# Triangle layers with channels innermost, a mask shared between two engines, packed expert weights

## The reference

```
x += triangle(L0)(ln(x));  t += experts(F0)(ln(t))     16 experts, each mixes its 8 best tokens of 512
x += triangle(L1)(ln(x));  t += recurrence(R1)(ln(t))  sigmoid(Wx + V y), batch norm first
x += row scan(SC)(ln(x));  t += recurrence(R2)(ln(t))  new row = row + relu(conv(previous))
x += triangle(L3)(ln(x));  t += experts(F3)(ln(t))     best 2 of 8 experts per token
```

```
a = sigmoid(zn @ Wga + bga) * (zn @ Wla + bla)      (L1: times mask[i, j] as well)
b = sigmoid(zn @ Wgb + bgb) * (zn @ Wlb + blb)      (L1: times mask[i, j] as well)
k[i, j, c] = sum over m of a[.., m, c] * b[.., m, c]
out = sigmoid(zn @ Wgo + bgo) * (layernorm(k) @ Wlo + blo)
```

## Time and profile before

| | us |
|---|---|
| median of three runs | 572.27 |
| lowest, highest | 569.99, 575.90 |
| the profiled execution, as timed | 572.75 |
| its span, first to last instruction | 570.9 |
| PE / DVE / ACT / POOL busy | 442.5 / 364.1 / 238.3 / 244.8 |

### The profile page before, as it was taken

One profiled execution on the slowest core, in us unless ns is written; L12 is line 12 of the kernel. 1 busy time (PEld: TensorE's weight loads), 2 busy tenths in 40 slices (PEclk: granted clock), 3 DMA queues, 4 the chain that ended last, 5 costly groups with the idle time before them and its releaser, 6 DMA issues.

```text
span 570.9 us, 8797 instructions
## 1 busy us (share of the span) xinstructions
PE 442.5 (78%) x3116; PEld 340.7 (60%) x3116; DVE 364.1 (64%) x1215; ACT 238.3 (42%) x573; POOL 244.8 (43%) x309
## 2 busy tenths in 40 slices
PE   3698876985898765997489976799589857909996
PEld 2356753674447642996279974499345756806664
DVE  4888584819795576006924458500978498398885
ACT  1487555311675554573620005476379533200000
POOL 2598196002483494000420004100359297119995
PEclk9989989768798989799669997899789985558999
DMA  9300000000000000000000000000000000001223
GB/s 165 71 2 1 1 1 1 1 2 0 1 1 1 2 0 1 1 1 2 1 1 2 1 1 1 1 2 1 1 1 2 0 2 1 0 0 20 38 38 56
DMA packets 34107, 6.04 MB, mean 11 GB/s; under 512 B 33644, under 2 KB 33772, under 8 KB 34029
## 3 DMA queue, kind: packets, MB, share of 16 engines
q1 hardware_dynamic: 34062, 5.46, 5.5%
HBM read 3.36 MB, written 2.10 MB: 10 GB/s over the span
## 4 chain that ended last, share of the span: by engine, by line
PE 49%; DVE 32%; POOL 9%; ACT 5%; issue 2%; DMA 1%; SPq 1%; DVEq 0%; POOLq 0%
PE psum L1283 7%; DVE moments L293 6%; DVE ab L672 5%; PE psum L1045 5%; PE psum L1044 5%; PE psum L557 4%; DVE ab L660 4%; PE psum L401 4%; POOL z L339 3%; POOL x_cols L737 3%; PE psum L1456 3%; POOL gate L732 3%; DVE z L303 3%; PE psum L1434 2%; PE psum L568 2%
## 5 line engine op out<-in xcount | busy, mean ns | idle before, releaser
L401 PE MATMUL psum<-ident,z 128*128 128x128 f32 x256 | 55.7, 360 | 42.2 <-POOL z L339 42.2
L401 PEld LDWEIGHTS psum<-ident,z 128*128 128x128 f32 x256 | 39.0, 185 | 70.3 <-POOL z L339 57.8
L527 PE MATMUL psum<-wp_L,z_t 64*128 64x320 f32 x384 | 66.8, 483 | 3.3 <-ACT z_t L324 2.1
L339 POOL TENSOR_TENSOR z<-z,stats 128x496 f32<-128x496 f32 (+1 forms) x40 | 41.5, 1038 | 59.2 <-DVE z L303 59.2
L293 DVE BATCH_NORM_STATS2 moments<-x_cols 128x6 f32<-128x64 f32 x448 | 61.8, 211 | 4.2 <-POOL x_cols L737 3.9
L324 ACT ACTIVATE z_t<-psum 128x512 f32<-128x512 f32 x56 | 40.1, 721 | 38.2 <-PE psum L401 37.9
L336 POOL MEMSET z<- 128x16 f32 x32 | 4.0, 127 | 117.5 <-DVE z L303 117.5
L527 PEld LDWEIGHTS psum<-wp_L,z_t 64*128 64x128 f32 x384 | 35.3, 199 | 30.2 <-issue 26.0
L339 POOL TENSOR_TENSOR z<-x_cols,stats 128x512 f32<-128x512 f32 x24 | 25.1, 1050 | 61.0 <-DVE stats L299 60.8
L1136 ACT ACTIVATE ab<-psum,mv 128x128 f32<-128x128 f32 x112 | 41.2, 368 | 19.2 <-PE psum L1045 8.7
L1045 PE MATMUL psum<-ab,R_vt 128*128 128x128 f32 x224 | 48.5, 300 | 0.0
(11 more groups left out here) (250 smaller groups left out, 927.2 us busy)
## 6 DMA issues: line engine op xcount, KB each, us to landing
x_cols<-in_x_dram SPq DMA_DIRECT2D x16, 128.0 KB, 3.0
out_dram<-x_cols SPq DMA_DIRECT2D x32, 64.0 KB, 1.9
par<-in_par_dram SPq DMA_DIRECT2D x1, 644.5 KB
w<-in_w_dram SPq DMA_DIRECT2D x1, 264.0 KB
w<-in_w_dram SPq DMA_DIRECT2D x1, 256.0 KB
mask<-in_mask_dram SPq DMA_DIRECT2D x1, 64.0 KB
row<-in_row_dram SPq DMA_DIRECT2D x1, 3.3 KB
w2l<-in_w2l_dram SPq DMA_DIRECT2D x1, 2.0 KB
```

The lines of the kernel that those rows point to most:

```text
L339: pool.tensor_tensor(Z4[:, r, :, 0:c], values[:, r, :, 0:c], RSTD[:, q].unsqueeze(3).to_broadcast([N, SQ, G, c]), ALU.mult).then_inc(L.s[" ...
L401: m = pe.transpose(bank(b % 2)[:, k * N:(k + 1) * N], block_of(Z)(4 * b + k), ident[:, :])
L527: m = pe.matmul(bank(slot_bank(s) + h, 2 * 5 * C), ZT[rows, s, :], wp[l][rows, :, :], start=True, stop=True)
```

## The change

Four things, in the diff below.

The triangle factors lie in two planes, a and b, each (g, s, c) with the channel innermost: DVE writes runs of 32 floats, and PE reads one channel of all (g, s) with a step of 32 floats. PSUM slots are addressed as four groups of 256 columns.

The triangle product is copied to PROD, which is the buffer `squares`, as (g, c, s) in runs of 32; the transposes read it with a step of 32 floats. The squares go to the b plane of `ab`.

In L1 DVE does two of the four groups with the mask as scalar; POOL multiplies the sigmoids of the other two groups by the mask in SIG (`mask_pool`), and DVE multiplies these 128 elements by the linear part in one instruction, after waiting for POOL. On POOL the 32 masks stand ahead of the eight pairs.

The first expert weights are packed four experts to 128 rows: four matmuls of four columns on a block-masked pooled matrix, after a bias matmul that opens the accumulation. The load is four DMAs and one for the bias.

```diff
...
+DVE_MASKS = G // 2
...
-PAR_LOADS = 16 * 4
+PAR_LOADS = 16 * (3 + G + 1)
...
+        PROD = SQR
+        SQUARES = AB[:, NC:2 * NC]
...
-        ABt = AB[:, :].rearrange("p (a c n) -> p a c n", a=2, c=C)
+        ABt = AB[:, :].rearrange("p (a n c) -> p a c n", a=2, c=C)
...
-        t1 = stage("L1", "norm weights ones tri", src=XC, scratch=XR, eps=0, e2=EPS)
+        t1 = stage("L1", "norm weights ones tri", "masked", src=XC, scratch=XR, eps=0, e2=EPS)
...
+        def product_of(t):
+            rows = t[:, :].rearrange("p (f s) -> p s f", s=S)
+            return lambda s: rows[:, s, :]
...
         def slot(s):
...
-            return PSUM[:, o:o + 2 * BANK].rearrange("p (h f) -> p h f", h=2)[:, :, 0:2 * 5 * C]\
-                .rearrange("p h (g w) -> p h g w", g=2)
+            return PSUM[:, o:o + 2 * BANK].rearrange("p (g f) -> p g f", g=G)[:, :, 0:5 * C]
...
                 for h in range(2):
...
-                    m = pe.matmul(bank(slot_bank(s) + h, 2 * 5 * C), ZT[rows, s, :], wp[l][rows, :, :],
-                                  start=True, stop=True)
+                    m = pe.matmul(slot(s)[:, 2 * h:2 * h + 2, :], ZT[rows, s, :], wp[l][rows, :, :], start=True, stop=True)
...
                 for k in range(4):
-                    m = pe.transpose(bank(b % 2)[:, k * N:(k + 1) * N], block_of(Z)(4 * b + k), ident[:, :])
+                    m = pe.transpose(bank(b % 2)[:, k * N:(k + 1) * N], product_of(PROD)(4 * b + k), ident[:, :])
...
         def k_copy(eng, L, b):
...
-            out = Z[:, :].rearrange("p (s g c) -> p c g s", g=G, c=C)[:, 4 * b:4 * b + 4]
-            src = bank(KB[b % 4]).rearrange("p (c g s) -> p c g s", c=4, g=G)
+            out = PROD[:, :].rearrange("p (g c s) -> p g c s", g=G, c=C)[:, :, 4 * b:4 * b + 4, :]
+            src = bank(KB[b % 4]).rearrange("p (c g s) -> p g c s", c=4, g=G)
...
             for s in range(S):
...
-                act.activation(GATE[:, s * GC:(s + 1) * GC].rearrange("p (h g c) -> p h g c", h=2, g=2),
-                               slot(s)[:, :, :, 4 * C:], ACT.Sigmoid).then_inc(L.s["gate"], 1)
+                act.activation(GATE[:, s * GC:(s + 1) * GC].rearrange("p (g c) -> p g c", g=G),
+                               slot(s)[:, :, 4 * C:], ACT.Sigmoid).then_inc(L.s["gate"], 1)
...
-                act.activation(SIG[:, s % SLOTS, :].rearrange("p (h g w) -> p h g w", h=2, g=2),
-                               slot(s)[:, :, :, 0:2 * C], ACT.Sigmoid).then_inc(L.s["sig"], 1)
+                act.activation(sigmoids(s), slot(s)[:, :, 0:2 * C], ACT.Sigmoid).then_inc(L.s["sig"], 1)
...
             def out_square(b):
...
-                act.activation(SQR[:, b * BANK:(b + 1) * BANK].rearrange("p (s h f) -> p h s f", s=4, h=2),
+                act.activation(SQUARES[:, b * BANK:(b + 1) * BANK].rearrange("p (s h f) -> p h s f", s=4, h=2),
...
+        def sigmoids(s):
+            return SIG[:, s % SLOTS, :].rearrange("p (g w) -> p g w", g=G)
+        def factors(t):
+            return t.rearrange("p g (a c) -> p g a c", a=2)
         def to_ab(s):
...
-            return AB[:, :].rearrange("p (w g s) -> p g s w", g=G, s=S)[:, :, s, :]
+            return AB[:, :].rearrange("p (a g s c) -> p s g a c", a=2, g=G, s=S)[:, s]
...
         def masked_product(dve, s):
...
-            for g in range(G):
-                w = slice(g * 2 * C, (g + 1) * 2 * C)
-                m = dve.scalar_tensor_tensor(out=to_ab(s)[:, g, :], in0=slot(s)[:, g // 2, g % 2, 2 * C:4 * C],
-                                             scalar=mask[:, g * S + s:g * S + s + 1], in1=SIG[:, s % SLOTS, w],
-                                             op0=ALU.mult, op1=ALU.mult)
-            m.then_inc(t1.s["lin"], 1)
+            linear, sig = factors(slot(s)[:, :, 2 * C:4 * C]), factors(sigmoids(s))
+            for g in range(DVE_MASKS):
+                dve.scalar_tensor_tensor(out=to_ab(s)[:, g], in0=linear[:, g], scalar=mask[:, g * S + s:g * S + s + 1],
+                                         in1=sig[:, g], op0=ALU.mult, op1=ALU.mult)
+            dve.wait_ge(t1.s["masked"], t1.at["masked"] + s + 1)
+            dve.tensor_tensor(to_ab(s)[:, DVE_MASKS:], linear[:, DVE_MASKS:], sig[:, DVE_MASKS:], ALU.mult)\
+                .then_inc(t1.s["lin"], 1)
+        def mask_pool(pool, s):
+            pool.wait_ge(t1.s["sig"], t1.at["sig"] + s + 1)
+            sig = sigmoids(s)[:, DVE_MASKS:]
+            ours = mask[:, :].rearrange("p (g s) -> p g s", g=G)[:, DVE_MASKS:, s:s + 1].to_broadcast([N, G - DVE_MASKS, 2 * C])
+            pool.tensor_tensor(sig, sig, ours, ALU.mult).then_inc(t1.s["masked"], 1)
...
         def tri_dve(dve, L, after):
             for s in range(S):
...
-                sig = SIG[:, s % SLOTS, :].rearrange("p (h g w) -> p h g w", h=2, g=2)
...
-                    dve.tensor_tensor(to_ab(s).rearrange("p (h g) w -> p h g w", h=2), slot(s)[:, :, :, 2 * C:4 * C], sig,
-                                      ALU.mult).then_inc(L.s["lin"], 1)
+                    dve.tensor_tensor(to_ab(s), factors(slot(s)[:, :, 2 * C:4 * C]), factors(sigmoids(s)), ALU.mult)\
+                        .then_inc(L.s["lin"], 1)
...
             def out_sum(b):
...
-                                  SQR[:, b * BANK:(b + 1) * BANK].rearrange("p (n c) -> p n c", c=C), AX.X, ALU.add)\
+                                  SQUARES[:, b * BANK:(b + 1) * BANK].rearrange("p (n c) -> p n c", c=C), AX.X, ALU.add)\
...
+            if L is t1:
+                pool.wait_ge(par_in, PAR_LOADS)
+                for s in range(S):
+                    mask_pool(pool, s)
...
-        w1 = sb("w1", [C + 1, E0, H0])
+        pool_g = sb("pool_g", [N, G, C])
+        w1 = sb("w1", [GC, E0 // G, H0])
+        w1_bias = sb("w1_bias", [E0, H0])
...
-        hid = sb("hid", [N, 2, E0])
+        hid = sb("hid", [N, E0])
+        pooled = sb("pooled", [GC, E0 // G, G])
...
-            pe.matmul(bank(6)[0:C, 264:264 + E0], pool32[:, :], d16[:, :], start=True, stop=True).then_inc(L.s["plt_ps"], 1)
+            pe.matmul(bank(6)[:, 264:264 + E0], pool_g[:, :, :], d16[:, :], start=True, stop=True).then_inc(L.s["plt_ps"], 1)
+            pe.wait_ge(par_in, PAR_LOADS)
+            pe.matmul(bank(2, E0), w1_bias[:, :], ident[0:E0, 0:E0], start=True, stop=False)
...
-            pe.wait_ge(L.s["pad"], L.at["pad"] + 2)
-            pe.wait_ge(par_in, PAR_LOADS)
-            for e in range(E0):
-                m = pe.matmul(bank(6)[:, 288 + e:289 + e], w1[:, e, :], hid[0:C + 1, 0, e:e + 1], start=True, stop=True)
+            for k in range(E0 // G):
+                m = pe.matmul(bank(2)[:, k * G:(k + 1) * G], w1[:, k, :], pooled[:, k, :],
+                              start=False, stop=(k == E0 // G - 1))
...
             for e in range(E0):
-                m = pe.matmul(bank(6)[0:C, 320 + e:321 + e], w2[:, e, :], hid[:, 1, e:e + 1], start=True, stop=True)
+                m = pe.matmul(bank(6)[0:C, 320 + e:321 + e], w2[:, e, :], hid[:, e:e + 1], start=True, stop=True)
...
-            act.activation(hid[:, 1, :], bank(6)[:, 288:288 + E0], ACT.Gelu).then_inc(L.s["h"], 1)
+            act.activation(hid[:, :], bank(2, E0), ACT.Gelu).then_inc(L.s["h"], 1)
...
         def f0_pool(pool):
...
-            pool.memset(hid[C:C + 1, 0, :], 1.0).then_inc(f0.s["pad"], 1)
-            pool.wait_ge(f0.s["pad"], 2)
...
-            dve.wait_ge(L.s["pad"], L.at["pad"] + 2)
+            dve.wait_ge(L.s["pad"], L.at["pad"] + 1)
...
-            dve.tensor_scalar(pool32[:, :], pool32[:, :], float(C), small[:, 7:8], ALU.mult, ALU.subtract)\
-                .then_inc(L.s["pl"], 1)
+            dve.tensor_scalar(pool_g[:, :, :], pool32[:, :].unsqueeze(1).to_broadcast([N, G, C]), float(C), small[:, 7:8],
+                              ALU.mult, ALU.subtract).then_inc(L.s["pl"], 1)
...
-            dve.tensor_scalar(hid[0:C, 0, :], bank(6)[0:C, 264:264 + E0], 1.0 / C, None, ALU.mult).then_inc(L.s["plt"], 1)
+            dve.scalar_tensor_tensor(out=pooled[:, :, :],
+                                     in0=bank(6)[:, 264:264 + E0].rearrange("p (k r) -> p k r", r=G), scalar=1.0 / C,
+                                     in1=m4[:, :].unsqueeze(1).to_broadcast([GC, E0 // G, G]), op0=ALU.mult, op1=ALU.mult)\
+                .then_inc(L.s["plt"], 1)
...
                 for g in range(G):
...
-            sp.dma_start(w1[:, :, :], w1_d).then_inc(par_in, 16)
+            for r in range(G):
+                sp.dma_start(w1[r * C:(r + 1) * C, :, :], w1_d[0:C, r:E0:G, :]).then_inc(par_in, 16)
+            sp.dma_start(w1_bias[:, :], w1_d[C:C + 1, :, :].rearrange("o e h -> (o e) h")).then_inc(par_in, 16)
...
```

## The result

The changed kernel takes 581.74 us (median, 579.38 to 582.36) beside 574.09 for the kernel before on the same chip: a ratio of 1.0123, interval 1.0075 to 1.017. It is slower by about 1.2%, where the forecast was 0.7% faster; the range of 563 to 574 did not hold it. The rival *strided moving reads* is what happened. The profiled execution took 582.36 us with a span of 580.6, 9.7 more than the span before.

What follows compares the result with a forecast made beforehand. No one engine bounds the kernel: PE sets L0's and L3's projection pace, DVE L1's. L0 -0.5, expert layer -4.6, L1 +1.0, L3 -0.5 sum to -4.6, taking 572.75 to 568.2 us; range 563 to 574.

Steps and rivals of the forecast that it cites:

- strided moving reads: Rival: triangle records go from 0.112 to 0.224 us, L0 and L3 each lose 7.2; +16.4, 584.6 us; chance 0.12.
- strided reads by PE: Triangle operands, kt transposes and L0's b turning read one float every 128 bytes; cost taken as zero, loaded or moving.
- the two gains of 0.5: L0 and L3: shorter last DVE product, 0.20, and last DVE copy, 0.34, gain 0.5 us each.
- the +1.2 for the pause: L1 output projections: after PE waits some 6 us for POOL, two blocks at clock 0.50 come late; +1.2 us.
- The step was put at 0.57 us: L1 projection: time per step falls from 0.772 to 0.57 us with half the masks on POOL.
- the last product at 5.0 us earlier: L1 projection: DVE's last product comes 5.0 us earlier, at 171.65 on the old time axis.
- the first gate multiplication at -0.2 us: L1: POOL's eight pairs queue behind the masks and eat the 5.0 us; first gate multiplication at 192.2 instead of 192.39.
- the term of -0.9: Expert layer: the 32 records after the packed matmuls come before the clock falls, about 0.95 us against 1.88.
- the case of -3: Expert layer: gain of 3 us instead of 4.6 if the clock falls as early relative to the work.
- 0.2 for the wider instructions: Expert layer: 128 columns instead of 32 add 0.1 us in the centred pool and 0.1 in its transposition.
- 0.34 for the copies: L0 and L3: only the last DVE product copy of each layer is on the path; its gain is 0.34 us.
- The other 0.2 of my 0.5, for the last product: L0 and L3: DVE's shorter product gains 0.2 us only at the last step, since PE sets the pace.

Runs made afterwards that it cites:

- first experiment: The changed kernel with the triangle factors back to channels outermost, so that PE reads contiguous rows, all else as changed: 571.37 us, ratio to before 0.9963.

## Why the prediction was wrong, and where it was right

**The step that failed: "strided reads by PE", taken as zero.** I priced the triangle's reads from 32 strided transpositions at 0.12 us a record. That row was read rightly but belongs to another operation: written as matmuls, strided loads double the records. For the moving operand the prediction said that no row shows it, and then took the end that the same row suggested. I kept 0.224 us as the upper end; 0.220 was measured. The Trainium skill, SBUF — State Buffer, in the section Specifications (TRN2), says that a 16-byte line wants two accesses for full rate. The traces agree for matmuls: a step of 8 bytes took 7.27 us, one of 16 bytes 14.52. They do not agree for transpositions, 1.13 us against 1.06. The prediction named this rule and gave it 0.12; evidence from the wrong kind of instruction outweighed it.

**The size of that rival.** It gave 584.6 us, 11.8 above the profiled execution of before; 9.6 was measured. What it said of L0 and L3 held: 13.6 us lost, for 14.4 less the two gains of 0.5. That its total came within 2.2 us is in part luck, since L1 came out better than it said and the expert layer worse. It let 2 us of an L1 triangle that is longer by 7.2 through. But L1's triangle had taken 9.05 us before, not 7.16, and now took 14.23: 5.2 longer. It ended at 190.3, and the first reciprocal behind it was done at 196.58, just as POOL's last pair ended (196.61 in the chain). So the two paths tie in this kernel, and 0.4 us came through. The long triangle also filled PE's pause: no output projection in L1 waited more than 1.67 us (7.10 with the masks alone), and the clock stayed at 1.00. So the +1.2 for the pause fell away: the eight gate multiplications spread over 20.6 us, against 22.3 where the triangle was short again.

**L1 was right where it was hard.** The step was put at 0.57 us and came to 0.58; the mask at 0.43 and 0.403; the last product at 5.0 us earlier and 4.5; the first gate multiplication at -0.2 us from the layer's start and +0.4. POOL's timeline shows the eaten gain, last mask, first pair, last pair, gate multiplication without a gap of note:

```profile
175.30 0.40 POOL L683 TENSOR_TENSOR sig<-sig,mask 128x128 f32<-128x128 f32 x1 [0.18 <-ACT sig L611]
175.66 1.28 POOL L656 TENSOR_TENSOR x_rows<-gate,bo_L 128x512 f32<-128x512 f32 x1
...
195.32 1.29 POOL L665 TENSOR_TENSOR x_rows<-x_rows,x_cols 128x512 f32<-128x512 f32 x1
196.72 1.05 POOL L755 TENSOR_TENSOR gate<-gate,stats 128x512 f32<-128x512 f32 x1
```

The 14.82 us of idle before it are gone, and nothing was won. In this kernel the doubled triangle would have held the gate multiplication as well; that POOL's pairs do it by themselves is shown by the kernel with contiguous factors (first experiment). The +1.2 for the clock after the pause, hidden in the changed kernel, showed in the masks alone (22.4 us for 21.2).

**The expert layer.** Eight records in 1.02 us for 0.95: right. The 32 records behind them took 1.80 us where I had 0.95: the term of -0.9 fell, since the granted clock went down as early relative to the work as before, which the prediction had named as the case of -3. In the changed kernel's profile the layer gained 2.0 us; alone, the edit gained 4.6 to 7.5 in the time. From the first packed matmul to the first output addition the layer is 3.9 us shorter (6.8 for 10.7). Ahead of that matmul it is 1.9 us longer, where I had 0.2 for the wider instructions: the clock had fallen earlier. From 4.3 to 6.3 us after the layer's start, before and changed:

```profile
102.70:104.70 2.00, 1.74 (x12) 1.53 (x13) 1.38 (x10) 1.65 (x4) 0.00 (x0) 1.00 0.00 0
```

```profile
108.60:110.60 2.00, 1.75 (x7) 1.69 (x8) 1.13 (x8) 1.40 (x4) 0.00 (x0) 0.50 0.00 0
```

**L0 and L3 without the stride.** Products and copies became as short as priced, and the pace of the projections stayed PE's. With contiguous factors the two layers gain 0.2 us each from the last product to the first gate multiplication, where I had 0.34 for the copies; the copies alone give the same 0.2. The other 0.2 of my 0.5, for the last product, no trace here can show: the start of L0 varies by more, and with contiguous factors the product still takes 608 ns.

## What to carry to other kernels

A layout that spares one engine's writes is paid for by whoever reads it: price the reader with a row of the same operation, for a transposition's load says nothing of a matmul's. If a float32 matmul must read strided, keep two neighbours in 8 bytes; here runs of two gave DVE all that runs of 32 gave, and cost PE 2 to 5% of its triangle. And before moving work onto an engine off the path, list what queues behind it: the masks, and the four pairs on DVE, each moved a wait without removing it.

## What the runs showed of the hardware beyond what I expected

- In L0, where only the moving operand steps, a float32 matmul record of 128 columns took 0.112 us at a step of 4 bytes, 0.114 at 8, 0.227 at 16 and 0.220 at 128. In L3, where both step, it took 0.116, 0.122, 0.241 and 0.223. The loaded or the moving operand alone was enough, and at 128 bytes both cost no more than one.
- A strided record did not mind the clock. In L3 of the changed kernel PE did as many records in 2 us at a granted clock of 0.50 as at 1.00; contiguous ones, in L1 before, ran at half the pace at 0.50 (0.213 us a record for 0.112). So at 0.50 a step of 128 bytes cost next to nothing (0.217 us for 0.213), and at 1.00 it doubled the record. L3 changed, then L1 before:

```profile
447.70:449.70 2.00, 2.00 (x11) 2.00 (x10) 0.56 (x1) 0.40 (x1) 0.94 (x1) 0.50 0.00 0
451.70:453.70 2.00, 2.00 (x11) 2.00 (x11) 0.01 (x1) 0.60 (x1) 0.00 (x0) 1.00 0.00 0
```

```profile
178.00:180.00 2.00, 2.00 (x11) 2.00 (x11) 0.00 (x0) 1.03 (x1) 0.00 (x0) 0.50 0.00 0
182.00:184.00 2.00, 2.00 (x20) 2.00 (x19) 1.04 (x1) 1.27 (x2) 0.00 (x0) 1.00 0.00 0
```

- A strided load cost a transposition 7% and the same data loaded for a matmul 91%.
- DVE's 256-element product took 608 ns with single elements at 512-byte steps and 425 in runs of two, four and 32 elements.
- POOL's pair instructions took 1.28 us beside DVE's products, as the earlier trace rows shows, but 1.59 to 1.73 beside the same instructions on DVE.
- Masked products of 64 elements fell from 320 to 275 ns with runs, and still two of them issued in 0.46 us: as in the earlier trace rows, the spacing of about 0.19 us does not follow the duration.
